# The stage that makes q, k and v: parts cut on VectorE and ScalarE, four stores per group, and first experts that write x + y

## What is computed

```
x = x + 0.5 * ffn(layernorm(x))
x = x + attention(layernorm(x))
x = x + 0.5 * ffn(layernorm(x))

ffn(x):        top1 = argmax(softmax(x @ router_w + router_b))     # 8 experts
               h = x @ w1[top1] + b1[top1];  a, g = split(h)       # 128 -> 2 x 512
               y = (a * sigmoid(g)) @ w2[top1] + b2[top1]
attention(x):  q, k, v = x @ w_qkv, 16 heads of 8 values
               attn = softmax(q k^T / sqrt(8) + phi_bias(1024))
               out = attn v @ w_proj + b_proj
```

## Time and profile before

| | us |
|---|---|
| median of three runs (range) | 1176.14 (1175.2 to 1176.85) |
| profiled execution | 1176.85 |
| its span | 1175.0 |
| VectorE busy | 919.6 (78%) |
| TensorE busy, matmul | 988.4 (84%) |
| ScalarE busy | 712.0 (61%) |
| GpSimd busy | 386.7 (33%) |

### The profile page before, as it was taken

One profiled execution on the slowest core, in us unless ns is written; L12 is line 12 of the kernel. 1 busy time (PEld: TensorE's weight loads), 2 busy tenths in 40 slices (PEclk: granted clock), 3 DMA queues, 4 the chain that ended last, 5 costly groups with the idle time before them and its releaser, 6 DMA issues. The chain is left out here.

```text
span 1175.0 us, 36380 instructions
## 1 busy us (share of the span) xinstructions
PE 988.4 (84%) x11682; PEld 554.5 (47%) x11683; DVE 919.6 (78%) x1749; ACT 712.0 (61%) x1542; POOL 386.7 (33%) x492
## 2 busy tenths in 40 slices
PE   5569993661799999999999999999999987729997
PEld 4469993330233333333333333333333336619996
DVE  6647774753999999999999999999999917737885
ACT  1034441341588888888888888888888871114443
POOL 2723433333232332332332233233233221533443
PEclk9999997775799999999999999999999997759999
DMA  9411113464122222222222222222222227332220
GB/s 324 150 37 46 39 43 86 119 179 133 34 64 74 71 62 70 62 70 66 69 72 57 72 61 74 66 67 70 61 71 62 66 72 260 113 113 66 65 69 26
DMA packets 78413, 99.29 MB, mean 85 GB/s; under 512 B 16731, under 2 KB 60385, under 8 KB 77712
## 3 DMA queue, kind: packets, MB, share of 16 engines
q1 hardware_dynamic: 72608, 87.41, 25.8%
q0 software_dynamic: 5056, 10.53, 2.5%
q10 hardware_dynamic: 704, 0.79, 0.3%
HBM read 69.02 MB, written 33.27 MB: 87 GB/s over the span
## 5 line engine op out<-in xcount | busy, mean ns | idle before, releaser
L984 DVE TENSOR_REDUCE nmax<-psS 128x1 f32<-128x1024 f32 x512 | 600.7, 1216 | 53.8 <-PE psS L924 48.5
L998 ACT ACTIVATE prob<-psE 128x512 f32<-128x512 f32 x1024 | 551.7, 598 | 114.3 <-PE psE L909 110.5
L909 PE MATMUL psE<-qop,kop 122*32 122x512 bf16 x4096 | 316.5, 385 | 10.7 <-ACT prob L998 4.5
L1039 POOL TENSOR_TENSOR prob<-prob,const 128x512 f32<-128x512 f32 x128 | 163.2, 1275 | 453.4 <-ACT prob L998 453.4
L942 PE MATMUL psV<-prob,vst 128*9 128x256 f32 x4096 | 265.6, 379 | 7.3 <-ACT osum L1006 6.9
L924 PE MATMUL psS<-maxop 32*128 32x512 bf16 x1024 | 167.3, 393 | 44.9 <-DVE mpart L967 25.7
L909 PEld LDWEIGHTS psE<-qop,kop 122*32 122x32 bf16 x4096 | 92.0, 95 | 153.2 <-ACT prob L998 72.8
L942 PEld LDWEIGHTS psV<-prob,vst 128*9 128x9 f32 x4096 | 102.0, 90 | 119.9 <-issue 15.9
L924 PEld LDWEIGHTS psS<-maxop 32*128 32x128 bf16 x1024 | 45.2, 91 | 194.5 <-issue 117.6
L751 ACT ACTIVATE siga<-psGa,w1sa 128x128 f32<-128x128 f32 x156 | 44.6, 368 | 63.4 <-PE psGa L659 63.4
L751 ACT ACTIVATE sigb<-psGb,w1sb 128x128 f32<-128x128 f32 x156 | 44.6, 368 | 60.6 <-PE psGb L659 60.6
(11 more groups left out here) (159 smaller groups left out, 952.4 us busy)
## 6 DMA issues: line engine op xcount, KB each, us to landing
maxop<-qk_parts SPq DMA_DIRECT2D x256, 64.0 KB, 2.2
qk_parts<-part_attend SPq DMA_DIRECT2D x80, 128.0 KB, 2.4
qop<-qk_parts SPq DMA_DIRECT2D x64, 144.0 KB
kop<-qk_parts SPq DMA_DIRECT2D x64, 144.0 KB
weighted_sums<-osum SPq DMA_DIRECT2D x64, 128.0 KB
xsb<-sorted_b SPq DMA_DIRECT2D x39, 128.5 KB, 2.0
w1a<-in_w SPq DMA_DIRECT2D x1, 4128.0 KB, 19.8
w1b<-in_w SPq DMA_DIRECT2D x1, 4128.0 KB, 14.3
```

The lines of the kernel that those rows point to most:

```text
L909: last = nc.tensor.matmul(psE[BANK[n]][32 * c:32 * c + 32, :], kop[b][0:TROWS, lo:lo + 32], qop[b][0:TROWS, half * HALF:(half + 1) * HALF] ...
L984: nc.vector.tensor_reduce(nmax[r % 2][:, qt:qt + 1], psS[n % 2][:], AX.XY, ALU.max, negate=True).then_inc(s_max, 1)
L998: nc.scalar.activation(prob[r % 2][:, lo:lo + HALF], psE[BANK[n]][:], ACT.Exp).then_inc(s_exp, 1)
L1039: nc.gpsimd.tensor_tensor(dst, dst, diag[:, 4 * h:4 * h + 4, :], ALU.mult).then_inc(s_diag, 1)
```

## The change

It rewrites the stage "attend" as a function of its own, `phase_attend`, and touches what feeds it and what reads its output.

1. Turn "a" uses rows of 257 values as turn "b" does, and its tokens stage loads x into them (in pieces of 512 B); the first experts add x and b2 to xb and so write x + 0.5 * y. `phase_attend` loads that into `g.x`, and GpSimd's addition is gone.
2. The scale of q goes into w_qkv, once, on VectorE. The low part is subtracted by VectorE instead of GpSimd, which has no instruction left in the stage.
3. On the host, the columns of w_qkv for q and k are ordered by dimension first, then head. `qk_parts` becomes [batch, slot, dim, head, q or k, token], and the partitions of a part then lie in equal steps of 4 KiB in DRAM. So one DMA stores two or three slots: four stores per group, 32 in all, with the same bytes.
4. The rows of one head lie 64 KiB apart in the new layout; the loads of `maxop`, `qop` and `kop` have the same sizes as before, and their address takes the batch's number too. `maxop` is loaded behind groups 2 to 5, `qop` and `kop` behind 6 and 7.

```diff
-ROW = {"a": D + 1, "b": 2 * D + 1}
+ROW = 2 * D + 1
-STORES = len(QSEQ) + len(KSEQ)
+STORES = 4
+DIMSTEP = HEADS * 2 * L
+SLOTSTEP = DH * DIMSTEP
+BATCHSTEP = len(KSEQ) * SLOTSTEP
...
+def phase_attend(nc, d, g):
...
+        @block.sync
+        def _(sp):
+            y = d.y.rearrange("(p t) d -> p (t d)", p=P)
+            for n in range(groups):
+                sp.dma_start(g.x[:, cols(n)], y[:, cols(n)]).then_inc(s_src[n], 16)
...
+            def store(n, z, slot, parts):
+                hi = part[:, n % 2, z, 0, :]
+                step = 0 if parts == "hh" else HALF
+                src = bass.AP(tensor=hi.tensor, offset=hi.offset, ap=[list(hi.ap[0]), [step, len(parts)], [1, HALF]])
+                to = bass.AP(tensor=d.qk.tensor,
+                             offset=n // 2 * BATCHSTEP + slot * SLOTSTEP + z * L + n % 2 * HALF,
+                             ap=[[2 * L, P], [SLOTSTEP, len(parts)], [1, HALF]])
+                sp.dma_start(to, src).then_inc(s_out[n % 2], 16)
+            for n in range(groups):
+                sp.wait_ge(s_lo, 2 * n + 1)
+                store(n, 0, 0, "hh")
+                store(n, 0, 2, "hml")
+                sp.wait_ge(s_lo, 2 * n + 2)
+                store(n, 1, 0, "hml")
+                store(n, 1, 3, "hm")
+                if n == 1:
+                    for s in range(2):
+                        sp.wait_ge(s_out[s], 16 * STORES)
+                if 2 <= n < 2 + NBUF:
+                    load_max_parts(sp, d, g, n - 2, 0, n - 2)
+                if n in (6, 7):
+                    load_parts(sp, d, g, n - 6, 0, n - 6)
```

```diff
-def load_max_parts(sp, d, g, head, b):
-        src = bass.AP(tensor=d.qk.tensor, offset=head * HEADSIZE + q,
-                      ap=[[2 * L, SROWS], [k - q, 2], [1, HALF]])
+def load_max_parts(sp, d, g, head, batch, b):
+    at = head * (2 * L) + batch * (BATCHSTEP - DIMSTEP)
+        src = bass.AP(tensor=d.qk.tensor, offset=at + q, ap=[[DIMSTEP, SROWS], [k - q, 2], [1, HALF]])
...
-                    if tag == "b":
-                        nc.vector.tensor_tensor(xb[:, (r + 1) % XBUF, :], g.b2[:, bass.ds(e * D, D)],
-                                                xs[:, (r + 1) % XBUF, D + 1:], ALU.add)
+                    nc.vector.tensor_tensor(xb[:, (r + 1) % XBUF, :], g.b2[:, bass.ds(e * D, D)],
+                                            xs[:, (r + 1) % XBUF, D + 1:], ALU.add)
...
-                    if tag == "a":
-                        e = expert(i - 1)
-                        more = g.b2[:, bass.ds(e * D, D)]
-                    else:
-                        more = xb[:, (r + 3) % XBUF, :]
-                        dve.drain()
+                    more = xb[:, (r + 3) % XBUF, :]
+                    dve.drain()
```

More of the change, by code:

```diff
@@ L78, in scatter_group @@
 def scatter_group(nc, pool, d, g, xn, n):
-    row = ROW[g.turn]
+    row = ROW
     for t in range(4 * n, 4 * n + 4):
@@ L183, in phase_tokens @@
             sem(n) for n in ("var", "std", "xn", "tp", "xT", "used"))
[L184 to L188, removed]
+        xn_rows = sb("xn", [P, NT * ROW])
+        xn = xn_rows[:].rearrange("p (t r) -> p t r", r=ROW)
+        xt = xn[:, :, D + 1:]
         s_src = [sem(f"src{n}") for n in range(groups)]
[L190 to L198, removed]
-        else:
[L200 to L207, removed]
+        psL = banks("psL")
+        logit, eq, row = (sb(n, [P, 2, 4, E]) for n in ("logit", "eq", "row"))
+        hot, upto = sb("hot", [P, 2, E, 5]), sb("upto", [P, 2, E, 5])
+        best, pick, posf = (sb(n, [P, 2, 4]) for n in ("best", "pick", "posf"))
+        s_upto, s_rank, s_read, s_pos = sem("upto"), sem("rank"), sem("read"), sem("pos")
+        plan = Plan(m, tag, psL[groups % 2])
         if last_part:
@@ L284, in _ @@
-            if not attend:
-                plan_padding(sp, d, g, plan, range(E // 2))
+            plan_padding(sp, d, g, plan, range(E // 2))
         @block.gpsimd
         def _(pool):
[L289 to L301, removed]
@@ L302, in _ @@
-            if not attend:
-                pool.wait_ge(g.s_put, 16 * NT)
+            for t in range(groups):
+                pool.wait_ge(s_pos, t + 1)
+                scatter_group(nc, pool, d, g, xn_rows, t)
+            pool.wait_ge(g.s_put, 16 * NT)
         @block.vector
@@ L341, in new_x @@
                         x.rearrange("p (j d) -> p j d", d=D), ALU.add).then_inc(s_x, 1)
[L343 to L351, removed]
             if first:
                 dve.wait_ge(s_small, 3 * 16)
-            if not attend:
-                nc.vector.tensor_copy(xn[:, :, D:D + 1], g.const[:, C_TOK:C_TOK + NT].unsqueeze(2))
+            nc.vector.tensor_copy(xn[:, :, D:D + 1], g.const[:, C_TOK:C_TOK + NT].unsqueeze(2))
             iota = g.const[:, C_IOTA:C_IOTA + E].unsqueeze(1).to_broadcast([P, 4, E])
@@ L363, in _ @@
                 turned, fresh = t + 1, t + 2
-                choose = not attend and live(t)
-                place = not attend and live(t - 1)
+                choose = live(t)
+                place = live(t - 1)
                 s, o = t % 2, (t + 1) % 2
@@ L517, in _ @@
                     use(t + 1)
-                if not attend and live(t):
+                if live(t):
                     rank(t)
@@ L1172 @@
     const[:, C_TILE:C_TILE + ET] = np.arange(ET) * P
+    w_qkv = np.asarray(L0_attn_w_qkv).copy()
+    by_dim = w_qkv[:, :2 * D].reshape(D, 2, HEADS, DH).transpose(0, 1, 3, 2)
+    w_qkv[:, :2 * D] = by_dim.reshape(D, 2 * D)
     def tiled(a):
```

254 lines of the change are left out of this document (159 added, 95 removed).

## The result

The changed kernel takes 1145.69 us (median of four runs, 1144.42 to 1146.33) against 1175.75 of the kernel before on the same chip: a ratio of 0.9742, 95% interval 0.9725 to 0.9759, 30 us faster. The forecast was 1150, so the direction and the place were right, and the gain was some 3.5 us larger than worked out. The span of the profiled execution fell from 1175.0 to 1144.5 us.

The account below looks back on a forecast made before the run. SyncE's issuing in the q, k, v stage was taken as the bound. Minus 26.2 there, minus 2.6 (first experts) and plus 2.1 (first tokens stage) made minus 26.7: 1150 us against 1176.14, own range 1144 to 1156.

Parts of the forecast that it names:

- The bound: q, k, v stage: SyncE's issuing ends last, not arithmetic or transfers; 80 stores are 51 us of its queue.
- Store issue: q, k, v stage: a merged store of two or three parts issues in 0.65 us (range 0.60 to 0.90).
- Rival A: q, k, v stage: SyncE's issue goes by parts, 1.9 us per three-part store; gain 4 to 5, 1171 us; chance 0.10.
- The period: q, k, v stage: VectorE's chain of work sets 6.5 us per group.
- The end: q, k, v stage: last low part at 254.9, last kop load ends at 258.0 against 284.2, minus 26.2 us.
- Clock: q, k, v stage: TensorE's lower clock costs 1.5 us on the whole stage (0 to 4).
- First experts: First experts' stage: becomes like the second, 38 intervals of y take 107.7 instead of 110.3 us, minus 2.6.
- First tokens stage: First tokens stage: 0.7 us for x in smaller pieces and 1.4 at the scatters' end, together plus 2.1.
- Attention: Attention loop: same transfers and sizes, 10.2 us per head; added register instructions costed at nothing (0 to 3 us).
- Rival C: Attention loop: loads with 64 KiB between rows land late, each head waits; 1 us per head gives 1214; chance 0.04.
- B: q, k, v stage: the DMA engines become the bound, stage ends at 263, 1155 us in all; chance 0.10.
- D: q, k, v stage: ScalarE, held by landing stores, sets 8 us per group instead of 6.5; 1162 us; chance 0.06.

Follow-up runs that it names:

- the repetition: The kernel before with the new layout and ten stores of one part, the store's address pattern written in two levels: 1166.24 us, ratio 0.9909.

## Why the prediction came out right

**The bound.** It was read rightly: SyncE's issuing ended last, and taking issues away moved the end. The two kernels between show how its 51 us of stores were made up. Over the stage, the layout alone takes it from 90.86 to 79.32 us (78.47 in the repetition), the merged stores from there to 73.44, and the wide rows, the scale in w_qkv and the emptied GpSimd to 63.07. (The stage lengths come from several chips; where a kernel ran on two, they differ by 0.2 to 0.9 us.) The prediction had only counted instructions: it saw no gain in the layout as such, and gave the whole to the number of stores. **That step was incomplete**, and its sum was right because the merged stores were priced near what they turned out to cost. That price was chosen between two rows of unlike DMAs, so there is luck in it.

**Store issue.** Taken 0.65, measured 0.53 (median); a group's four take 2.4 us instead of 2.6. They are not alike: the first, of two parts, takes 0.37 to 0.51 us, the two of three parts 0.47 to 0.64, and the last, of two parts again, 0.69 to 1.01. Rival A, issue by parts, is out: 0.64 is far from 1.9. (Its own sum was off by two: 65 us from 213 on end at 278, not 280.)

**The period.** Predicted 6.5, measured 6.03, in the order that was described: normalise 1.11, low parts 1.29 (1.3 taken), the wait between rests and reciprocal 0.79 (0.95 taken). The 0.45 too much is spread over the links, since I added durations where neighbours overlap. Statistics start 1.03 us after the normalisation's 1.11 (220.10 to 221.13), the rests 1.47 after the statistics where I had 1.57, the normalisation 1.21 after the low parts, and from rests to reciprocal it is 2.07 instead of 2.24. Over five periods this is 2.3 us.

**The end.** The last low part was predicted at 254.9 and the kop load's end at 258.0, with the stage starting at 194.3. Measured, with a start at 190.48, they are 246.5 and 252.46; with both starts taken off, 60.6 against 56.0 and 63.7 against 62.0. The arithmetic was 4.6 us earlier than worked out: 1.6 until the first group's low parts (208.11), 2.3 in five periods and 1.5 for the clock, less 0.8 in the last two groups, where ScalarE waited 1.03 us for a buffer, a wait that the prediction had taken as covered (its 4.5 us of transfers per group are 4.9 by the earlier trace rows). The end was only 1.7 earlier: SyncE is in the way again. Group 7's first low part is done at 245.85, but the loads behind group 6 (245.52 to 247.41) hold back its stores by 1.5 us, and two more loads follow the stores. The stores and loads behind the last low part took 6.0 us, where 3.1 had been taken. Moving the loads gave 3.5 us. The prediction had one line for this end and didn't look at what stood in the queue ahead of it.

**Clock.** 1.5 us were set aside. The granted clock of the new stage from 216 to 246 us is 1.00, 0.83 and 1.00 in windows of 10 us, against 0.80 before from 246 to 256. TensorE's two levels show in the pair of rows for q and k, 1.98 and 3.78 us, and in no steady period did TensorE set the pace: the turn in which q and k took 3.54 us (at 228.64) lasted 6.04 us, like its neighbours. The half microsecond that the lower clock was to cost did not appear.

**First experts.** Predicted -2.6; the 38 intervals of y take 106.5 us, so -3.8, and the second stage, unchanged, 107.6. The 1.2 beyond the forecast is open: over these intervals TensorE is busy 104.9 us in the first stage and 106.0 in the second, at a granted clock of 1.00 in both, and no run tells why.

**First tokens stage.** Predicted +2.1, measured -0.1: **the one term that was wrong in its sign**. Loads of x in pieces of 512 B arrive no later (first statistics 5.59 against 5.89), and from the last scatter to the experts' first instruction it is 5.66 us against 5.44, not the 1.4 more that I read out of the second turn. The 0.7 for the smaller pieces had no row behind it. The 1.4 came from a difference that the width of the rows doesn't make: in the changed kernel both turns have the same width, and the second still takes 7.18 us (1011.66 to 1018.84). What makes it is open.

**Attention.** Predicted 0, measured +0.7 over 64 heads, of which VectorE's reductions and their waits carry 0.8 (601.2 + 54.1 against 654.5). Rival C, late loads with rows 64 KiB apart, is out: maxop lands in 1.9 us instead of 2.2.

**The other rivals.** B, the DMA engines: their share rose to 0.89 without setting the period; how near they come to it once VectorE's wait is gone stays open. D, ScalarE held by stores: a single wait of 1.0 us in the changed kernel, but 10.5 us in the kernel before, 13.2 with ten stores and 5.2 with the root first, so the mechanism is real, and with the changed kernel's order of work the merged stores keep it away. The power-of-two pitch of 512 KiB between a store's parts that the Trainium skill warns of ("DMA: Bandwidth & Descriptors", section "Latency and other measured facts") cost nothing that these runs show: 273 GB/s in the window above, against 178 with the old layout. That is no test of it. The 207 GB/s that the Trainium skill gives there were measured with that pitch between partitions, which here lie 4 KiB apart, and no run has the same stores at another pitch.

## What to carry to other kernels

When a DMA queue is what ends last, three things shorten it: fewer instructions, a layout in which one instruction is cheaper to issue, and order, since anything not yet needed should stand behind what the next stage waits for or on another queue. Price an issue from a row of the same shape and layout, not of the same size. And when an engine leaves the path, look at what it really overlapped: a subtraction of GpSimd that covered part of VectorE's normalisations cost them 0.84 us, and 1.72 when both started together.

## What the runs showed of the hardware that I had not expected

- SyncE's time to issue a DMA depends on where its rows lie. A store of 128 pieces of 1 KB: 0.60 us in the old layout, 0.45 in the new. A maxop load, whose pattern has the same levels and counts in both: 0.60 with rows 4 KiB apart, 0.35 to 0.37 with rows 64 KiB apart. It isn't so for every DMA: the one maxop load of four that has 32 pieces of 2 KB takes 0.32 to 0.33 us in both layouts, and the load of kop 0.86 and 0.85. The cause is open; the run that was to separate levels from addresses couldn't.
- A store of two or three parts (256 or 384 pieces) issues in 0.37 to 0.64 us when it is among the first three of its group, little more than one of a single part (0.45). The fourth in a row takes 0.69 to 1.01.
- Issues behind a group's merged stores are slow: four maxop loads take 2.7 us there, the first alone 1.04 to 1.07, and in these 2.8 us the DMA share is 1.02 to 1.05 (222.0 to 224.8 and the like). Behind single stores in the same layout they take 1.87 us at a share of 0.7, and 1.8 in the loop at 0.23. Full DMA engines are the likely reason, but single issues of 1.65 to 2.2 us also stand where the share is 0.3 to 0.4, and no run explains them.
- Four normalisations on VectorE take 1.11 us alone, 1.95 beside a GpSimd subtraction that overlaps them for 1.35 us, 2.83 where both start together (2.2 us of overlap), and 3.78 beside a subtraction and an addition.
